# A graph attention layer: a chunk's two sorting stages at one place of VectorE's step, or at two

## What is computed

```python
n_in, n_out = node[recv], node[send]
wn_out = n_out @ W_lin + b_lin
e_ij = leaky_relu(concat([n_in, n_out]) @ W_att + b_att)       # slope 0.2
a_ij = (e_ij @ w_alpha)[:, 0]
seg_max = segment_max(a_ij, recv)
a_exp = exp(a_ij - seg_max[recv])
alpha = a_exp / maximum(segment_sum(a_exp, recv)[recv], 1e-12)
n_i = segment_sum(alpha[:, None] * wn_out, recv)
out = layernorm(x + elu(n_i))
```

## Time and profile before

| | us |
|---|---|
| median of 3 runs | 2309.03 |
| lowest and highest of them | 2305.78, 2310.81 |
| the profiled execution | 2305.88 |
| its span, first to last instruction | 2304.2 |
| busy in it: TensorE / VectorE / ScalarE / GpSimd | 1788.3 / 1756.8 / 1462.2 / 1621.2 |

### The profile page before, as it was taken

How to read it: one execution, slowest core, us unless ns; L and a number is a source line. 1 busy time by engine, 2 the same in 40 slices (tenths; PEclk the granted TensorE clock), 3 DMA queues, 4 the chain that set the end, 5 groups by cost and what they waited for, 6 DMA issues and landing times.

```text
span 2304.2 us, 62973 instructions
## 1 busy us (share of the span) xinstructions
PE 1788.3 (78%) x11697; PEld 1446.5 (63%) x11697; DVE 1756.8 (76%) x5206; ACT 1462.2 (63%) x4913; POOL 1621.2 (70%) x1669
## 2 busy tenths in 40 slices
PE   5648787888888888887778887878878787878770
PEld 2336666766666766676666666666667666666660
DVE  9848977887689778786888887878766666666667
ACT  2336677876667666675666666666666666666665
POOL 2057777777777777777777777777777777777760
PEclk9869999999999999999999999999999999999995
DMA  3145555455455555554555455555555555555541
GB/s 120 60 105 136 135 130 134 131 132 139 128 135 133 130 130 134 131 139 127 134 131 133 129 135 132 130 129 134 134 135 135 135 134 135 133 136 135 133 111 56
DMA packets 165719, 294.14 MB, mean 128 GB/s; under 512 B 40002, under 2 KB 110014, under 8 KB 165329
## 3 DMA queue, kind: packets, MB, share of 16 engines
q0 software_dynamic: 78864, 216.03, 36.3%
q1 hardware_dynamic: 85733, 73.82, 12.6%
q10 hardware_dynamic: 732, 0.27, 0.1%
HBM read 278.95 MB, written 11.02 MB: 126 GB/s over the span
## 4 chain that ended last, share of the span: by engine, by line
POOL 22%; issue 12%; PE 10%; DMA 7%; DVE 3%; ACT 1%; DVEq 1%; POOLq 0%; ACTq 0%
POOL rows L639 22%; DMA rows<-qv_table,senders 7%; PE turned_ps L970 2%; PE hidden_ps L944 2%; PE masked_ps L955 2%; PE hidden_ps L942 2%; PE turned_ps L962 1%; PE masked_ps L954 1%; DVE sums L1531 1%; DVE leaky L1487 0%; DVE spare L1622 0%; DVEq L1531 0%; DVE x_sb L1617 0%; ACT x_sb L842 0%; DVE sums L1607 0%
## 5 line engine op out<-in xcount | busy, mean ns | idle before, releaser
L639 POOL DMA_INDIRECT rows<-qv_table,senders x1635 | 1593.9, 975 | 505.2 <-issue 463.3
L942 PE MATMUL hidden_ps<-identf,rows 128*128 128x128 f32 x1635 | 462.8, 283 | 342.3 <-DMA rows<-qv_table,senders 333.4
L1531 DVE SCALAR_TENSOR_TENSOR sums<-sums,shrink,turned_ps 128x129 f32 x1660 | 571.9, 345 | 78.9 <-issue 26.1
L970 PEld LDWEIGHTS turned_ps<-rows,spare 128*128 128x128 f32 x3270 | 438.6, 192 | 283.5 <-ACT spare L766 209.6
L751 ACT ACTIVATE spare<-masked_ps,peaks 128x128 f32<-128x128 f32 x1660 | 472.7, 368 | 221.3 <-DVE peaks L1509 217.1
L944 PE MATMUL hidden_ps<-onehotT,p_unit 128*128 128x128 f32 x3320 | 593.8, 281 | 0.0
L1494 DVE TENSOR_REDUCE lows<-masked_ps 128x4 f32<-128x512 f32 x415 | 286.1, 689 | 400.4 <-PE masked_ps L955 399.2
L944 PEld LDWEIGHTS hidden_ps<-onehotT,p_unit 128*128 128x128 f32 x3320 | 525.1, 199 | 0.4 <-issue 0.4
L970 PE MATMUL turned_ps<-rows,spare 128*128 128x129 f32 x3270 | 469.1, 279 | 50.8 <-DVE sums L1531 45.6
L942 PEld LDWEIGHTS hidden_ps<-identf,rows 128*128 128x128 f32 x1635 | 236.9, 145 | 392.6 <-issue 363.1
L741 ACT ACTIVATE sloped<-hidden_ps 128x512 f32<-128x512 f32 x415 | 249.0, 600 | 363.5 <-PE hidden_ps L944 354.6
(11 more groups left out here) (195 smaller groups left out, 857.6 us busy)
## 6 DMA issues: line engine op xcount, KB each, us to landing
lanes_all<-lane_list SPq DMA_DIRECT2D x415, 128.0 KB
single_rows<-qv_table SPq DMA_DIRECT2D x3200, 1.0 KB
rows<-qv_table,senders POOLq DMA_INDIRECT x1635
qv_table<-rows SPq DMA_DIRECT2D x24, 257.0 KB, 2.7
out<-x_sb SPq DMA_DIRECT2D x1, 1344.0 KB
out<-x_sb SPq DMA_DIRECT2D x1, 896.0 KB
kept<-windows SPq DMA_DIRECT2D x3, 208.0 KB
out<-x_sb SPq DMA_DIRECT2D x1, 448.0 KB
```

Of the source, the lines that this page charges most:

```text
L639: g.indirect_dma_start(out=rows[:, k % U, c, :], out_offset=None, in_=table, in_offset=bass.IndirectOffsetOnAxis(ap=senders[:, s % 2, c * ...
L942: t.matmul(whole[:, unit], rows_at_unit(k, c)[:, 0:F], identf[:], is_transpose=True, start=True, stop=False, skip_group_check=True)
L970: mm = t.matmul(unit_sums_ps[:, c, :], weights[:, k % 2, c * P:(c + 1) * P], rows_at_unit(k, c)[:, F:R], start=True, stop=True)
L1531: v.scalar_tensor_tensor(out=at, in0=at, scalar=shrink[:, k % 4, i:i + 1], in1=unit_sums_ps[:, i, :], op0=ALU.mult, op1=ALU.add).then_inc( ...
```

## The change

The generator of the sort now yields behind every stage. Behind the first of two stages it yields the word `HALF`; `besides(k)` notes that, and a new function `second_half()`, called in VectorE's `step(k)` between `make_onehot(k+5)` and sum 3, lets the generator do the second. Stages that stand alone, at the end of a run with an odd number, yield no `HALF`, and neither do the calls of counting, padding and gaps. The assertion on the count of steps is fitted to it. In which chunk a stage is done doesn't change; p stays in fp32.

```diff
+            HALF = "half of a step"
+
             def sort_in_loop(s):
...
                     done, now = done + 1, 1 - now
-                    if n % 2:
-                        yield
+                    yield HALF if n % 2 == 0 else None
...
-                            assert steps == run_ends[s][run] and now == (SORTED[s] if run == runs_of(s) - 1 else ends_in[run])
-                        if n % 2 or n == stages - 1:
-                            yield
+                            assert steps - (n % 2) == run_ends[s][run] and now == (SORTED[s] if run == runs_of(s) - 1 else ends_in[run])
+                        yield HALF if n % 2 == 0 and n < stages - 1 else None
...
-            sorting_now, steps = None, 0
+            sorting_now, steps, half_done = None, 0, False
+
+            def second_half():
+                nonlocal half_done
+                if half_done:
+                    next(sorting_now)
+                half_done = False
 
             def besides(k):
-                nonlocal sorting_now, steps
+                nonlocal sorting_now, steps, half_done
...
                     if SORT_FROM[s] <= k <= SORTED_AT[s]:
-                        next(sorting_now)
+                        half_done = next(sorting_now) == HALF
                         steps += 1
...
                 if k + 5 < NCH:
                     make_onehot(k + 5)
+                second_half()
                 add_sums(k, 3, of)
```

## The result

| | before | after |
|---|---|---|
| median of 7 runs, us | 2309.03 | 2316.88 |
| lowest and highest | 2305.78, 2315.13 | 2311.4, 2320.97 |
| the profiled execution / its span | 2305.88 / 2304.2 | 2315.32 / 2313.6 |
| ratio, 95% interval | | 1.0036 (1.0024 to 1.0048) |

The account below looks back on a forecast made before the run. GpSimd's gathers bound the kernel: 136.8 us ahead, 2102.2 us stream and 65.2 us behind make a 2304.2 us span; all change terms were 0, so the forecast was the earlier median, 2309.0 us, range 2298 to 2320.

Parts of the forecast that it names:

- The bound: GpSimd's 1635 gathers set the span, a 2102.2 us stream never held by the ring of eight row buffers.
- Counts and VectorE's time: No instruction added or removed; 18 us of VectorE's time moves into its wait for masked scores, worth 0.
- the stage wait: Second sorting stage's wait for the first's end on VectorE, 0.11 us in each of 163 chunks, would go.
- The growth and one-hot that come sooner: With sum 2, 0.79 us earlier on VectorE; worth 0 because GpSimd never waits for the ring.
- The term for windows met: Reordered compares and one-hots hold starting gathers differently in 163 sorting chunks: -2.6 to +10 us, taken as 0.
- rival B: Held gathers sit out a whole unbroken run of locking VectorE instructions: +35 us, 2344 us, chance 0.05.
- Rival A: Moved second pair of compares lands where released gathers fall into its windows: +10 us, 2319 us, chance 0.18.

Follow-up runs that it names:

- growth_between_3: Growth and one-hot exchanged against the change, so growth stands between one-hot and second pair of compares; ratio 0.9997 to the kernel before.
- second profile: The change run once more with nothing edited, against the kernel before; ratio 1.0027.
- pair_behind_reduce: Against the kernel before: first pair of compares directly behind the reduce, second behind the leaky maximum, one-hot behind sum 3; ratio 0.9904, 2285.04 us.
- behind_sum3_3: Second pair of compares moved behind sum 3, against the change; ratio 1.0028 to the kernel before.
- first eight runs: Two batches of four reordered kernels, the change among them, run where GpSimd also waits for the sums; the kernel before took 3244.58 and 3305.05 us.
- change_again: The change again with nothing edited, in the first batch, against the kernel before; ratio 1.004.
- first four runs: First batch: the change again, second pair behind sum 3, growth and one-hot exchanged, one-hot ahead of four unsplit compares; kernel before 3244.58 us.

## Why the prediction was wrong, point by point

- **The bound** was right: GpSimd's stream of gathers, never held by the ring, sets the span. Prologue and tail didn't move, and every ratio that moved did so by the gathers' length.
- **Counts and VectorE's time** were right: no instruction more, the stage wait gone (the compares of the second stage now follow the one-hot by 0.40 us), and VectorE's wait for the masked scores up, in the sorting piece from 64.1 to 73.0 us, in the whole span from 399.2 to 427.6. Worth nothing, as said. The growth and one-hot that come sooner were worth nothing either.
- **The term for windows met** (-2.6 to +10 us, taken as 0) was about right in its sum: outside the long gathers the stretch went from 46.7 to 41.9 us. Had each of the 19 long gathers been let go at the window's end, after some 0.2 us, it would be 46 us by my estimate: -1 us. That the sum is near nothing was partly luck, as two large moves cancel, +10 us in compares and -8 in one-hots (growth_between_3, where the compares stand as in the change).
- **The step that failed** is the one that left joined holds out of the sum and made them rival B, at 5% and 35 us. What they took is 14.2 us more than before, less the 4 us that the same gathers would have been held anyway by that estimate: some +10 us, which is the whole result. Some 9 of it is in the 13 joined holds in one-hots. Parting one-hot and compare, with the compares left in place, took it away (growth_between_3, +0.5 us). I judged B by the rate of joins in the trace of before ("joins are rare"). But no gather there could show the new case: the one-hot was always followed by a sum, and the sorting compares always began behind the leaky maximum. The change put a compare directly behind the one-hot, with growth and a sum ahead, and that pair joins in 9 of the 10 gathers that start 0.08 to 0.18 us into it and in 2 of the 11 that start 0.18 to 0.21 us into it. The pair of leaky maximum and first compare did stand in the kernel before, in which none of 33 such gathers joined; in the change 5 of 49 do, in its second profile none of 43. An operation's price was taken from rows in which it had another neighbour.
- **Rival A's price** (+10 us; given as 2319 us, and as 2320 at the range's end) agrees with the result by chance; its mechanism isn't it, as growth_between_3 shows with the compares at the same places.
- The page of the Trainium skill that I set beside B ("SBUF — State Buffer", section "SBUF: two separate sides": locked for the full instruction, the loser fully blocks) was nearer than I allowed. A single hold ends at 0.34 us of a 0.48 us one-hot, short of the page's rule. A joined hold lasts past the one-hot's end, to 1.03 us, which the page doesn't describe either.

What remains open is the state that lets a hold join, for one-hots and for compares, and the place of pair_behind_reduce among better orders: four orders that gain were run, and no search was made.

## What to carry to other kernels

When one engine's stream sets the time and another only disturbs it, cost a reordering by who becomes whose neighbour, and ask whether the trace of before shows that pair at all; if not, its price is not bounded by the rows at hand. Here VectorE works from SBUF to SBUF beside GpSimd's indirect DMAs, and a short instruction between two locking ones parted them at no cost (growth_between_3, 0.9997). A sum between them parted the one-hot from the compares too, but then the compares joined among themselves (behind_sum3_3, 1.0028), so each order has to be run. Most of the largest gain (1%) came with one move, the one-hot to behind the last sum (0.7%). Compare the stream engine's longest instruction before and after (1452 against 1884 ns): that one number pointed at the mechanism. It doesn't give the price: growth_between_3 has a longest gather of 1807 ns and costs nothing, for there are only 2 over 1.4 us. Count them.

## What the runs showed that I had not expected

- A gather that starts 0.10 to 0.18 us into a one-hot with compares behind it is held either to 0.35 us or to about 1.02 us behind its start, with nothing between; whether the long hold occurs depends on the instruction ahead, by two runs in which only that was exchanged (ratio 0.9966 against 1.0068).
- Between two compares the same happens on a smaller scale: 66 gathers of 1.25 to 1.4 us in behind_sum3_3. Before there are 4, of which only 1 starts in a compare; the other 3 start in the counting of what is left over.
- Orders of the same instructions have spans from 2283.3 to 2316.1 us, 1.4% apart.
- Beside the first eight runs the kernel before took 3244.58 and 3305.05 us. In change_again ScalarE waits 795.0 us in 135 cases there for a signal whose source the trace doesn't show. The chip alone doesn't explain it: the record gives the first four runs and growth_between_3, beside which the kernel before took 2307.14 us, the same chip number. The cause is open.
